# One attention stage in place of three: gathered rows kept in SBUF, softmax in blocks of seven items, radial network in the last stage

## The chip, the cores and the metric

The kernel runs on one core of one Trainium2 chip. The metric is device microseconds of one execution, the median over runs. The core's engines are TensorE (PE), VectorE (DVE), ScalarE (ACT), GpSimd (POOL, which issues the indirect DMAs) and SyncE (SP, which issues the plain ones). Each runs its own instructions in order; they meet only at semaphores.

## The reference

Four graph layers over 100,000 nodes of 128 numbers and 50,000 edges, each followed by a residual sum and a layer norm. Layer 1 (the attention) and layer 3 (the radial network) are what the change touches:

```python
# layer 1, per edge: score, softmax over the edges of one receiver, weighted sum
e = jnp.sum(Q[receiver] * K[sender], axis=-1) * scale
m = jax.ops.segment_max(e, receiver, num_segments=num_nodes)
w = jnp.exp(e - m[receiver])
denom = jax.ops.segment_sum(w, receiver, num_segments=num_nodes)
numer = jax.ops.segment_sum(w[:, None] * V[sender], receiver, num_segments=num_nodes)
return x + numer / denom @ Wo
...
# layer 3, per edge: a small network of the edge's length gives 4 x 32 weights for its message
h = jax.nn.silu(emb @ mlp_w0 + mlp_b0)
h = jax.nn.silu(h @ mlp_w1 + mlp_b1)
w = (h @ mlp_w2 + mlp_b2).reshape(-1, 4, MUL)
...
m0 = w[:, 0] * ss                                  # and m1, m2, m3, from w, the sender's row and the edge's direction
msg_s = jax.ops.segment_sum(mid_s, receivers, num_segments=num_nodes)
```

The edges come sorted by receiver, so a sum or a maximum over one receiver's edges is a scan along the edges that restarts where the receiver changes.

## The kernel before, in words

The edges are padded to 392 chunks of 128. Four chunks are an *item* (98 items), two items are an *eight* or a *pair* (49). The kernel is a row of stages, with a barrier of all engines between them: `prepare`, `scores_and_sort`, `gat_softmax`, `gat_sums`, `first_layer`, `attention_scores`, `attention_softmax`, `second_layer`, `gcn_first`, `gcn_second`, `final_edges`.

Inside a stage each engine runs `pipeline(engine, (f, lag), ...)`: in *slot* s it calls the listed functions in their order, each f for item s - lag. There is no scheduler; this order in a slot, the lags and the semaphores alone decide who waits for whom. `wait_item(engine, sems, t, u, back)` makes a step of item q wait until item q - back has passed a semaphore, which is how a buffer is protected: back 2 for two buffers, back 1 for one.

- `attention_scores` (tiles `asc_`): per item POOL gathers four chunks of sender rows (L1554), PE turns and multiplies the receiver rows (L1584, L1591), DVE takes their product with the gathered rows (`dot`, L1643 to L1648), SP stores the gathered rows to the table `xsrc`. Beside this the radial network is computed: PE `first`, `second`, `third` (L1597, L1603, L1610), two Silu on ACT (L1628, L1633), DVE `keep` (L1653), and a store to the table `radial`.
- `attention_softmax` (`asm_`): the softmax over all 50,176 scores at once, through a table in DRAM; meanwhile the line of flags `cont` (1 where an edge has the same receiver as the one before it) is broadcast into all partitions as `K["cont"]`.
- `second_layer` (`ats_`): per eight SP loads the rows of `xsrc`, POOL weights them (L1764), PE turns them, DVE scans (L1812), PE multiplies (L1785), ACT copies out, POOL adds the node's own row (L1769), DVE and ACT do the layer norm (`norm_measure`, `norm_root`, `norm_scale`, `apply`).
- `final_edges` (`mss_`): per item POOL gathers four chunks (L2110) and, 15 slots later, scatters four chunks to the output (L2102). ACT scales, PE turns (L2123), ACT copies, PE projects into `up` (L2130), DVE makes messages (`messages`, L2191 to L2198) with the weights loaded from `radial`, PE turns them (L2138), ACT copies them (`copy_msg`, L2173), PE reduces (L2145), DVE scans (L2205), PE turns back into `op` (L2152), DVE combines (L2211) and norms.

In `final_edges` the orders in a slot are, before the change:

```python
pipeline(pe, (turn_x, 1), (turn_back, 9), (project, 3), (reduce, 7), (turn_sums, 5))
pipeline(act, (copy_x, 2), (copy_msg, 6), (lambda t, u: norm_root(norm, act, t, u), 11), (scale_x, 0),
         (lambda t, u: norm_apply(norm, act, t, u, scattered, 64), 12))
pipeline(dve, (scan, 8), (messages, 4), (combine, 10), (lambda t, u: norm_scale(norm, dve, t, u), 11))
```

Of the kernel before, what the change touches and what calls it, by code (L numbers as in the profile page):

```python
# [20 lines left out]
P = 128  # L21
N = 100000
# [1499 lines left out]
def attention_scores(nc, A, T, K):  # L1522
    with ExitStack() as ctx:
        sb, ps, sem, sems, owned = stage_makers(nc, ctx, "asc")
        xs = [sb(f"xs{u}", [P, 4, ROW1]) for u in range(BUFS)]
        xd = [sb(f"xd{u}", [P, 4, D]) for u in range(BUFS)]
        xdT = [sb(f"xdT{v}", [P, 4, P]) for v in range(2)]
        prod = [sb(f"prod{u}", [P, 4, D]) for u in range(BUFS)]
        four_scores = [sb(f"fs{u}", [P, 4]) for u in range(BUFS)]
        scores = sb("scores", [P, CHUNKS])  # L1530
        rows = sb("rows", [P, 4, P])
        h1 = [sb(f"h1{v}", [P, 2, P]) for v in range(2)]
        h2 = [sb(f"h2{v}", [P, 2, P]) for v in range(2)]
# [4 lines left out]
        sT = ps("sT", [P, 4, P])
        loaded, gathered, turned, copied = sems("loaded"), sems("gathered"), sems("turned"), sems("copied")
        multiplied, dotted, kept, stored = sems("multiplied"), sems("dotted"), sems("kept"), sems("stored")  # L1540
        h1_ready, h1_done, h2_ready, h2_done = sems("h1_ready"), sems("h1_done"), sems("h2_ready"), sems("h2_done")
        wp_ready, w_ready, w_stored = sems("wp_ready"), sems("w_ready"), sems("w_stored")
        all_scored, scores_turned, rows_ready, rows_stored = sem("all_scored"), sem("scores_turned"), sem("rows_ready"), sem("rows_stored")
        block = ctx.enter_context(nc.Block())

        @block.gpsimd
        def _(pool):
            for q in range(ITEMS):
                t, u = q // BUFS, q % BUFS
                wait_item(pool, kept, t, u, 4)  # L1550
                wait_item(pool, stored, t, u, 4, 16)
                for j in range(4):
                    c = 4 * q + j
                    pool.indirect_dma_start(xs[u][:, j, :], None, T["t12"][0:EP + N],  # L1554
                                            bass.IndirectOffsetOnAxis(K["idx_a"][:, c:c + 1], 0)).then_inc(gathered[u], 16)

        @block.sync
        def _(sp):
            def store(t, u):
                sp.wait_ge(gathered[u], 64 * t + 64)  # L1560
                sp.dma_start(tile_rows(T["xsrc"], t, u), as_tile_rows(xs[u][:])).then_inc(stored[u], 16)

            def load(t, u):
                wait_item(sp, turned, t, u, 4)
                sp.dma_start(xd[u][:], part_rows(T["t12"][0:EP], t, u)).then_inc(loaded[u], 16)

            def store_w(t, u):
# [756 lines left out]
```

## Time and profile before

| what | us |
|---|---|
| median of 3 runs (lowest, highest) | 5378.56 (5373.77, 5383.27) |
| the profiled execution, its own time | 5376.34 |
| its span, first to last instruction | 5374.6 |
| `attention_scores` (2490 to 2989 in the span) | 499 |
| `attention_softmax` (2989 to 3023) | 34 |
| `second_layer` (3023 to 3321) | 298 |
| `gcn_first` (3321 to 3829) | 508 |
| `final_edges` (4353 to 5374) | 1021 |

The stages are cut at the first and last instruction on their own tiles. In a table of stretches, "busy" is the union of an engine's instructions, so an engine may be busy half of a stage and still set its pace through one chain; the busy shares say which engine cannot be the limit, the waits and the order of time say which is. Times in the timelines are us from the span's start; an instruction's duration may overlap the start of the next on its engine by about a tenth, so what a step costs is read from start to start.

### The profile page before, as it was taken

What the parts mean: (1) busy time and instruction counts of PE and PEld (TensorE: products, weight loads), DVE (VectorE), ACT (ScalarE), POOL (GpSimd) and SP (SyncE); (2) the same over time, 40 slices, a digit from 0 to 9 for tenths busy, and PEclk for the clock granted to TensorE, in tenths of its full rate; (3) what the DMA queues carried; (4) which work ended last, traced back from release to release, by engine and by line L of the source; (5) the groups of instructions that cost most, each with busy time, mean ns of one, the idle gap of its engine ahead of it and who ended that gap; (6) DMA issues with size and microseconds to landing.
All of it is one profiled execution on the core that took longest, in us unless ns stands there. A gap on an engine that the chain in (4) does not pass through costs nothing. (4 is left out here: it accounts for less than half of the span.)

```text
span 5374.6 us, 74716 instructions
## 1 busy us (share of the span) xinstructions
PE 3172.1 (59%) x15690; PEld 2478.5 (46%) x15690; DVE 3358.4 (62%) x11850; ACT 2679.9 (50%) x6869; POOL 3855.3 (72%) x3733
## 2 busy tenths in 40 slices
PE   3536555545534664465777465666788866655564
PEld 3536545524323442355666454455455544444442
DVE  6587555568877775575333696333477767666665
ACT  0106666648866886385222375333355554444443
POOL 5777777667766777487777576777677767777777
PEclk9555555579977887798999787888655578888887
DMA  2327777768845775366777786777677643333332
GB/s 73 77 73 225 241 239 238 227 152 250 251 145 160 225 225 180 113 205 194 212 213 214 243 286 206 210 212 212 180 209 208 204 134 101 98 97 98 97 97 74
DMA packets 846208, 953.70 MB, mean 177 GB/s; under 512 B 161164, under 2 KB 570097, under 8 KB 845827
## 3 DMA queue, kind: packets, MB, share of 16 engines
q1 hardware_dynamic: 730304, 765.68, 44.9%
q0 software_dynamic: 112896, 179.36, 14.4%
q10 hardware_dynamic: 2882, 7.36, 0.4%
q8 instruction: 33, 0.54, 0.0%
q14 instruction: 93, 0.76, 0.0%
HBM read 534.20 MB, written 423.34 MB: 178 GB/s over the span
## 5 line engine op out<-in xcount | busy, mean ns | idle before, releaser
L1035 POOL DMA_INDIRECT t_alpha<-gsm_raw,gsm_edge_idx x392 | 386.2, 985 | 165.7 <-issue 118.3
L2110 POOL DMA_INDIRECT mss_xs<-t_x,kept_idx_a x392 | 377.9, 964 | 143.9 <-issue 119.1
L2102 POOL DMA_INDIRECT out_dram<-mss_o,kept_scat_idx x392 | 395.0, 1008 | 119.4 <-issue 117.9
L534 POOL DMA_INDIRECT sort_xd<-in_x_dram,kept_dst_idx x392 | 379.2, 967 | 140.3 <-issue 118.5
L1966 POOL DMA_INDIRECT gs_xs<-t_z,kept_idx_a x392 | 380.5, 971 | 137.5 <-issue 119.2
L1025 POOL DMA_INDIRECT gsm_raw<-t_al,kept_idx_b x392 | 378.2, 965 | 124.1 <-issue 118.9
L1554 POOL DMA_INDIRECT asc_xs<-t_t,kept_idx_a x392 | 370.0, 944 | 134.2 <-issue 110.3
L1856 POOL DMA_INDIRECT gs_xs<-t_t,kept_idx_b x392 | 370.0, 944 | 133.2 <-issue 119.2
L536 POOL DMA_INDIRECT sort_xs<-in_x_dram,kept_src_idx x392 | 379.7, 969 | 119.4 <-issue 118.5
L1227 PE MATMUL gsm_hp<-kept_w,gsm_zT 128*128 128x128 f32 x1568 | 254.9, 311 | 353.5 <-ACT gsm_zT L1093 353.4
L216 PE MATMUL gs_tp<-kept_ident,gs_xs 128*128 128x128 f32 x784 | 271.6, 364 | 250.9 <-DMA gs_xs<-t_t,kept_idx_b 185.1
L1227 PEld LDWEIGHTS gsm_hp<-kept_w,gsm_zT 128*128 128x128 f32 x1568 | 214.6, 212 | 404.1 <-ACT gsm_zT L1093 404.0
L2162 ACT ACTIVATE mss_xk<-mss_xs 128x128 f32<-128x128 f32 x392 | 125.2, 390 | 515.8 <-DMA mss_xs<-t_x,kept_idx_a 515.8
L1433 ACT ACTIVATE gsm_o<-gsm_y,gsm_nb,gsm_rs 128x128 f32<-128x128 f32 x784 | 323.7, 490 | 24.9 <-issue 24.6
L755 PE MATMUL sort_tpd<-kept_ident,sort_xd 128*128 128x128 f32 x392 | 108.9, 433 | 384.7 <-DMA sort_xs<-in_x_dram,kept_src_idx 384.7
L1923 DVE TENSOR_TENSOR_SCAN gs_sc<-kept_cont,gs_sc,gs_tp 128x512 f32<-128x512 f32 (+1 forms) x98 | 125.4, 1279 | 308.8 <-PE gs_tp L217 308.8
L1433 ACT ACTIVATE sort_o<-sort_x,sort_nb,sort_rs 128x128 f32<-128x128 f32 x792 | 312.3, 489 | 0.0
L2123 PE MATMUL mss_xtp<-kept_ident,mss_xk 128*128 128x128 f32 x392 | 82.9, 350 | 382.7 <-ACT mss_xsT L2168 361.5
L216 PEld LDWEIGHTS gs_tp<-kept_ident,gs_xs 128*128 128x128 f32 x784 | 145.5, 186 | 352.1 <-DMA gs_xs<-t_t,kept_idx_b 223.6
L2205 DVE TENSOR_TENSOR_SCAN mss_sc<-kept_cont,mss_sc,mss_rp 128x512 f32<-128x512 f32 (+1 forms) x98 | 125.4, 1279 | 280.8 <-PE mss_rp L2145 280.7
L793 ACT COPY sort_al<-sort_sps 128x16 f32<-128x16 f32 x98 | 16.8, 171 | 551.0 <-PE sort_sps L765 551.0
L1912 ACT ACTIVATE gs_o<-gs_hp,kept_dlast2B 128x128 f32<-128x128 f32 x392 | 112.1, 369 | 313.6 <-PE gs_hp L1897 313.5
(536 smaller groups left out, 11243.8 us busy)
## 6 DMA issues: line engine op xcount, KB each, us to landing
t_t<-sort_o SPq DMA_DIRECT2D x66, 792.0 KB
t_x<-gsm_o SPq DMA_DIRECT2D x196, 264.0 KB
sort_x<-in_x_dram SPq DMA_DIRECT2D x66, 768.0 KB
gsm_x<-t_t SPq DMA_DIRECT2D x196, 256.0 KB
t_z<-gsm_z SPq DMA_DIRECT2D x196, 256.0 KB
out_dram<-gsm_o SPq DMA_DIRECT2D x196, 256.0 KB
t_t<-l_o SPq DMA_DIRECT2D x49, 528.0 KB, 3.1
t_xsrc<-asc_xs SPq DMA_DIRECT2D x98, 264.0 KB, 2.3
```

The costliest lines, as they stand in the source:

```text
L216: pe.matmul(out, lhsT=a, rhs=ident[:], start=True, stop=False, is_transpose=True)
L534: pool.indirect_dma_start(xd[u][:, j, :], None, A["x"], bass.IndirectOffsetOnAxis(K["dst_idx"][:, c:c + 1], 0)).then_inc(gathered[u], 16)
L536: pool.indirect_dma_start(xs[u][:, j, :], None, A["x"], bass.IndirectOffsetOnAxis(K["src_idx"][:, c:c + 1], 0)).then_inc(gathered[u], 16)
L1025: pool.indirect_dma_start(raw[:, c, 0:HEADS], None, T["al"], bass.IndirectOffsetOnAxis(from_idx[:, c:c + 1], 0)).then_inc(gathered[u], 16)
L1035: pool.indirect_dma_start(T["alpha"], bass.IndirectOffsetOnAxis(edge_idx[:, c:c + 1], 0), raw[:, c, :], None).then_inc(scattered[u], 16)
L1227: mm = pe.matmul(hp[u % 2][:, j, :], zT[u][:, j, :], K["w1"][:], start=True, stop=True)
L1433: ac = act.activation(norm["o"][u][:, g, :], norm["y"][u][:, g, :], ACT.Identity, bias=norm["nb"][u][:, g:g + 1], scale=norm["rs"][u][:, g ...
L1554: pool.indirect_dma_start(xs[u][:, j, :], None, T["t12"][0:EP + N], bass.IndirectOffsetOnAxis(K["idx_a"][:, c:c + 1], 0)).then_inc(gathere ...
L1856: pool.indirect_dma_start(xs[u][:, j, :], None, T["t12"], bass.IndirectOffsetOnAxis(K["idx_b"][:, c:c + 1], 0)).then_inc(gathered[u], 16)
L1966: pool.indirect_dma_start(xs[u][:, j, :], None, T["z1"], bass.IndirectOffsetOnAxis(K["idx_a"][:, c:c + 1], 0)).then_inc(gathered[u], 16)
L2102: pool.indirect_dma_start(T["out"], bass.IndirectOffsetOnAxis(K["scat_idx"][:, c:c + 1], 0), o[u][:, j, :], None, bounds_check=N - 1, oob_ ...
L2110: pool.indirect_dma_start(xs[u][:, j, :], None, T["x3"], bass.IndirectOffsetOnAxis(K["idx_a"][:, c:c + 1], 0)).then_inc(gathered[u], 16)
```

## The change

Three stages become one, `attention` (tiles `att_`), and the radial network moves into `final_edges`.

- The gathered rows stay in a ring of 20 tiles `xs`; `xsrc` is neither stored nor loaded. POOL only gathers.
- The softmax runs in 14 blocks of seven items. In each, eight small steps on DVE alternate with six on PE and one Exp on ACT, one step per slot, with a running maximum and a running sum carried from block to block.
- The aggregation (weight, turn, scan, multiply, combine, norm) runs 16 slots behind the gather. Weighting is on ACT (was on POOL), adding the own row is on DVE (was on POOL), in one instruction per chunk with the division by the denominator.
- `in_slots` replaces `pipeline` there: parts are (f, lag, every, count).
- `K["cont"]` is filled in `gcn_first`, by four broadcasts on ACT's queue, and `gcn_first` loads its own flags item by item.
- In `final_edges` the three PE steps, the two Silu and `keep` join the slot; the load of `radial` goes. To make room in PSUM, `op` and `up` have one buffer each instead of two, so `turn_back` waits for the combine of the item before (back 1, was 2) and `project` for the messages of the item before (back 1, was 2).

The diff, cut to its core:

```diff
+BLOCK = 7
+RING = 20
+FIRST_STEP = BLOCK + 1
+WEIGHT_LAG = FIRST_STEP + 8
+def in_slots(*parts):
+    for s in range(max(lag + every * (count - 1) for _, lag, every, count in parts) + 1):
+        for f, lag, every, count in parts:
+            if s >= lag and (s - lag) % every == 0 and (s - lag) // every < count:
+                f((s - lag) // every)
...
+# attention: PE
+            in_slots((turn_weights, FIRST_STEP + 7, BLOCK, BLOCKS), (turn_scores, FIRST_STEP + 1, BLOCK, BLOCKS),
+                     (turn_tops, FIRST_STEP + 2, BLOCK, BLOCKS), (turn_carried_tops, FIRST_STEP + 3, BLOCK, BLOCKS),
+                     (turn_sums, FIRST_STEP + 5, BLOCK, BLOCKS), (turn_carried_sums, FIRST_STEP + 6, BLOCK, BLOCKS),
+                     (attend, WEIGHT_LAG + 2, 1, ITEMS), (multiply, 1, 1, ITEMS), (turn, 0, 1, ITEMS),
+                     (turn_weighted, WEIGHT_LAG, 1, ITEMS))
+# attention: ACT
+            in_slots((exponents, FIRST_STEP + 4, BLOCK, BLOCKS), (weight, WEIGHT_LAG, 1, ITEMS), (copy, 0, 1, ITEMS),
+                     (root, WEIGHT_LAG + 4, 2, PAIRS), (apply, WEIGHT_LAG + 5, 2, PAIRS))
+# attention: DVE
+            in_slots((take_weights, FIRST_STEP + 7, BLOCK, BLOCKS), (dot, 2, 1, ITEMS), (scan, WEIGHT_LAG + 1, 1, ITEMS), (combine, WEIGHT_LAG + 2, 1, ITEMS),
+                     (measure, WEIGHT_LAG + 3, 2, PAIRS), (scale, WEIGHT_LAG + 4, 2, PAIRS),
+                     (find_flags, FIRST_STEP, BLOCK, BLOCKS), (scan_tops, FIRST_STEP + 1, BLOCK, BLOCKS), (scan_row_tops, FIRST_STEP + 2, BLOCK, BLOCKS),
+                     (shift, FIRST_STEP + 3, BLOCK, BLOCKS), (scan_sums, FIRST_STEP + 4, BLOCK, BLOCKS),
+                     (scan_row_sums, FIRST_STEP + 5, BLOCK, BLOCKS), (invert_sums, FIRST_STEP + 6, BLOCK, BLOCKS))
...
 # gcn_first
+            part = EP // 4
+            for k in range(4):
+                act.dma_start(K["cont"][:, k * part:(k + 1) * part], T["cont"][0:1, k * part:(k + 1) * part].broadcast_to([P, part])).then_inc(cont_loaded, 16)
...
 # final_edges
-        op = [ps(f"op{v}", [P, 4, D]) for v in range(2)]
+        op = ps("op", [P, 4, D])
+        hp, wp = ps("hp", [P, 4, P]), ps("wp", [P, 4, D])
-        up = [ps(f"up{v}", [P, 4, D]) for v in range(2)]
+        up = ps("up", [P, 4, D])
             def project(t, u):
                 pe.wait_ge(x_copied[u], t + 1)
-                wait_item(pe, msg_ready, t, u, 2)
+                wait_item(pe, msg_ready, t, u, 1)
             def turn_back(t, u):
                 pe.wait_ge(scanned[u], t + 1)
-                wait_item(pe, combined, t, u, 2)
+                wait_item(pe, combined, t, u, 1)
+            def radial_first(t, u):
+                wait_item(pe, h2_done, t, u, 1)
+                for pair in range(2):
+                    mm = pe.matmul(hp[:, pair, :], K["m0g"][:, 2 * (u % 2) + pair, :], radial_block(K, t, u), start=True, stop=True)
+                mm.then_inc(h1_ready[u], 1)
-            pipeline(pe, (turn_x, 1), (turn_back, 9), (project, 3), (reduce, 7), (turn_sums, 5))
+            pipeline(pe, (radial_second, 1), (turn_x, 1), (turn_back, 9), (project, 3), (radial_third, 2), (radial_first, 0), (reduce, 7), (turn_sums, 5))
+            def radial_one(t, u):
+                act.wait_ge(h1_ready[u], t + 1)
+                act.activation(h1[u % 2][:], hp[:, 0:2, :], ACT.Silu, bias=K["mb0"][:, 0:1]).then_inc(h1_done[u], 1)
-            pipeline(act, (copy_x, 2), (copy_msg, 6), (lambda t, u: norm_root(norm, act, t, u), 11), (scale_x, 0),
+            pipeline(act, (radial_two, 1), (copy_x, 2), (radial_one, 0), (copy_msg, 6), (lambda t, u: norm_root(norm, act, t, u), 11), (scale_x, 0),
                      (lambda t, u: norm_apply(norm, act, t, u, scattered, 64), 12))
-            pipeline(dve, (scan, 8), (messages, 4), (combine, 10), (lambda t, u: norm_scale(norm, dve, t, u), 11))
+            pipeline(dve, (scan, 8), (messages, 4), (keep, 3), (combine, 10), (lambda t, u: norm_scale(norm, dve, t, u), 11))
```

The order on ACT in one slot of `final_edges`, before the change (`mss_xsT` is `copy_x`, `mss_mT` `copy_msg`, `mss_sd` the norm's root, `mss_xk` `scale_x`, `mss_o` the norm's apply):

```order
L2168 COPY mss_xsT<-mss_xtp 128x512
L2173 COPY mss_mT<-mss_tp 128x512 x2
L1408 ACTIVATE mss_sd<-mss_mv,kept_eps 128x4
L2162 ACTIVATE mss_xk<-mss_xs 128x128 x4
L1433 ACTIVATE mss_o<-mss_y,mss_nb,mss_rs 128x128 x4
```

and after it (L2247 is `radial_two`, L2242 `radial_one`):

```order
L2247 ACT_TABLE_LOAD
L2247 ACTIVATE mss_h<-mss_hp,kept_mb 128x256
L2233 COPY mss_xsT<-mss_xtp 128x512
L2242 ACTIVATE mss_h<-mss_hp,kept_mb 128x256
L2238 COPY mss_mT<-mss_tp 128x512 x2
L1408 ACT_TABLE_LOAD
L1408 ACTIVATE mss_sd<-mss_mv,kept_eps 128x4
L2227 ACTIVATE mss_xk<-mss_xs 128x128 x4
L1433 ACTIVATE mss_o<-mss_y,mss_nb,mss_rs 128x128 x4
```

Silu and the root alternate in every slot now, and each of the two is preceded by a load of ACT's function table; `radial_one` stands ahead of `copy_msg` and of the root.

The order on PE in one slot of `final_edges`, before (`mss_xtp` is `turn_x`, `mss_op` `turn_back`, `mss_up` `project`, `mss_rp` `reduce`, `mss_tp` `turn_sums`):

```order
L2123 MATMUL mss_xtp<-kept_ident,mss_xk 128x128 x4
L2152 MATMUL mss_op<-kept_ident,mss_sc 128x128 x4
L2130 MATMUL mss_up<-kept_wup,mss_xsT 128x128 x4
L2145 MATMUL mss_rp<-mss_mT,kept_wout 128x512 x2
L2138 MATMUL mss_tp<-kept_ident,mss_msg 128x128 x8
```

and after (L2210 is `radial_second`, L2217 `radial_third`, L2205 `radial_first`):

```order
L2210 MATMUL mss_hp<-mss_h,kept_m 128x256
L2171 MATMUL mss_xtp<-kept_ident,mss_xk 128x128 x4
L2200 MATMUL mss_op<-kept_ident,mss_sc 128x128 x4
L2178 MATMUL mss_up<-kept_wup,mss_xsT 128x128 x4
L2217 MATMUL mss_wp<-kept_m,mss_h 128x256 x2
L2205 MATMUL mss_hp<-kept_emb,kept_m0g 128x128 x2
L2193 MATMUL mss_rp<-mss_mT,kept_wout 128x512 x2
L2186 MATMUL mss_tp<-kept_ident,mss_msg 128x128 x8
```

`radial_third` and `radial_first` stand between `project` and `reduce`, behind `turn_back`, which waits for DVE.

## Rows read from the trace of the kernel before

**Rows 1.** Part 1 of the page: busy time and share of each engine

```profile
PE 3172.1 (59%) x15690; PEld 2478.5 (46%) x15690; DVE 3358.4 (62%) x11850; ACT 2679.9 (50%) x6869; POOL 3855.3 (72%) x3733
```

**Rows 2.** Stretches by stage: length, busy of each engine, TensorE clock, DMA share, GB/s

```profile
2490.00:2989.00 499.00, 357.71 (x2160) 314.78 (x2160) 182.80 (x1079) 140.90 (x295) 370.03 (x392) 0.92 0.75 210
2989.00:3023.00 34.00, 4.92 (x12) 2.17 (x12) 18.41 (x41) 1.81 (x2) 0.00 (x0) 0.50 0.53 207
3023.00:3321.00 298.00, 175.90 (x1176) 164.08 (x1176) 258.74 (x935) 210.91 (x491) 206.24 (x98) 0.83 0.79 267
4353.00:5374.00 1021.00, 584.27 (x2744) 441.81 (x2744) 627.33 (x2059) 438.80 (x1176) 772.88 (x784) 0.82 0.33 96
```

**Rows 3.** Part 5 of the page, costliest groups: busy, mean ns, idle before, releaser

```profile
L2110 POOL DMA_INDIRECT mss_xs<-t_x,kept_idx_a x392 | 377.9, 964 | 143.9 <-issue 119.1
L2102 POOL DMA_INDIRECT out_dram<-mss_o,kept_scat_idx x392 | 395.0, 1008 | 119.4 <-issue 117.9
...
L1554 POOL DMA_INDIRECT asc_xs<-t_t,kept_idx_a x392 | 370.0, 944 | 134.2 <-issue 110.3
```

**Rows 4.** Timeline of DVE, early in the final stage (start, duration)

```profile
4419.95 1.28 DVE L2205 TENSOR_TENSOR_SCAN mss_sc<-kept_cont,mss_sc,mss_rp 128x512 f32<-128x512 uint8 x1
...
4424.02 0.68 DVE L2211 TENSOR_TENSOR mss_y<-mss_y,mss_op 128x512 f32<-128x512 f32 x1
...
4426.26 0.17 DVE L1419 RECIPROCAL mss_rs<-mss_sd 128x4 f32<-128x4 f32 x1
...
4426.58 1.28 DVE L2205 TENSOR_TENSOR_SCAN mss_sc<-kept_cont,mss_sc,mss_rp 128x512 f32<-128x512 uint8 x1
```

**Rows 5.** Timeline of PE, and DVE's next scan, one slot of the final stage

```profile
4709.35 1.06 PE L2123 MATMUL mss_xtp<-kept_ident,mss_xk 128*128 128x128 f32 x4 [4.24 <-ACT mss_xsT L2168]
...
4710.20 1.06 PE L2152 MATMUL mss_op<-kept_ident,mss_sc 128*128 128x128 f32 x4
...
4711.05 1.90 PE L2130 MATMUL mss_up<-kept_wup,mss_xsT 128*128 128x128 f32 x8
...
4712.76 1.91 PE L2145 MATMUL mss_rp<-mss_mT,kept_wout 128*128 128x512 f32 x4
...
4714.79 1.28 DVE L2205 TENSOR_TENSOR_SCAN mss_sc<-kept_cont,mss_sc,mss_rp 128x512 f32<-128x512 f32 x1 [3.63 <-PE mss_rp L2145]
```

**Rows 6.** Groups of the old attention_scores: `keep` on DVE, Silu on ACT

```profile
L1653 DVE TENSOR_TENSOR asc_w<-asc_wp,kept_mb 128x512 f32<-128x512 f32 x98 | 67.6, 690 | 27.1 <-PE asc_wp L1610 20.1 <-issue 6.3
...
L1628 ACT ACTIVATE asc_h<-asc_hp,kept_mb 128x256 f32<-128x256 f32 x98 | 46.5, 474 | 95.6 <-PE asc_hp L1597 94.7 <-issue 0.9
```

**Rows 7.** Timeline of PE, radial third and first in the old attention_scores

```profile
2605.98 1.28 PE L1610 MATMUL asc_wp<-kept_m,asc_h 128*128 128x256 f32 x4 [1.91 <-DVE asc_w L1653]
...
2613.65 0.61 PE L1597 MATMUL asc_hp<-kept_emb,kept_m0g 128*128 x4
```

**Rows 8.** Timeline of ACT around a table load, in gat_softmax

```profile
1739.83 0.58 ACT L1088 COPY gsm_xT<-gsm_tp 128x512 f32<-128x512 f32 x1
1740.43 1.28 ACT L1433 ACT_TABLE_LOAD   x1
1741.72 1.65 ACT L1433 ACTIVATE gsm_o<-gsm_y,gsm_nb,gsm_rs 128x128 f32<-128x128 f32 x4
```

**Rows 9.** Timeline of ACT, copy of the messages and root, final stage

```profile
4424.24 1.08 ACT L2173 COPY mss_mT<-mss_tp 128x512 f32<-128x512 f32 x2
4426.38 0.30 ACT L1408 ACTIVATE mss_sd<-mss_mv,kept_eps 128x4 f32<-128x4 f32 x1 [1.07 <-DVE mss_mv L1399]
```

**Rows 10.** Timeline of DVE, first and last of a dot, old attention_scores

```profile
2702.91 0.29 DVE L1643 CUSTOM_DVE_ANT_0 asc_prod<-asc_qp,asc_xs 128x128 f32<-128x128 f32 x1 [1.69 <-DMA asc_xs<-t_t,kept_idx_a]
...
2704.10 0.17 DVE L1648 TENSOR_TENSOR asc_scores<-asc_fs,asc_xs 128x4 f32 x1
```

**Rows 11.** Timeline of DVE, one eight of second_layer

```profile
3150.35 1.64 DVE L1382 BATCH_NORM_STATS2 ats_small<-ats_y 128x6 f32<-128x128 f32 x8
...
3153.07 2.35 DVE L1812 TENSOR_TENSOR_SCAN ats_sc<-kept_cont,ats_sc,ats_tp 128x1024 f32<-128x1024 f32 x1
...
3155.94 1.64 DVE L1382 BATCH_NORM_STATS2 ats_small<-ats_y 128x6 f32<-128x128 f32 x8
```

More of the change, by code:

```diff
@@ L1538, in attention_scores @@
[L1538 to L1543, printed above, removed]
+        block_scores = [sb(f"bs{v}", [P, ROWS]) for v in range(2)]
@@ L1792, in apply, with exponents, root @@
+            def exponents(b):
+                act.wait_ge(soft_v, V_STEPS * b + 4)
+                act.activation(e[:], shifted[:], ACT.Exp).then_inc(exped, 1)
+            def root(p):
+                norm_root(norm, act, p // BUFS, p % BUFS)
+            def apply(p):
+                t, u = p // BUFS, p % BUFS
                 act.wait_ge(norm["scale_ready"][u], t + 1)
@@ L1815, in measure, with dot @@
-            def measure(t, u):
-                dve.wait_ge(summed[u], t + 1)
-                norm_measure(norm, dve, t, u)
-            def scale(t, u):
+            link = chain_of(dve, chain_v)
+            def dot(q):
+                dve.wait_ge(multiplied, q + 1)
+                dve.wait_ge(gathered[q % RING], 64 * (q // RING) + 64)
+                rows = xs[q % RING]
+                for j in range(4):
+                    dt = dve.tensor_tensor_reduce(prod[q % 2][:, j, :], qp[q % 2][:, j, :], rows[:, j, 0:D], 1.0, 0.0, ALU.mult, ALU.add,
+                                                  four_scores[q % BUFS][:, j:j + 1])
+                dt.then_inc(dotted, 1)
+                dve.wait_ge(dotted, q + 1)
+                dve.tensor_copy(kB[:, 4 * q:4 * q + 4], rows[:, :, D])
+                place = 4 * (q % BLOCK)
+                dve.tensor_tensor(block_scores[q // BLOCK % 2][:, place:place + 4], four_scores[q % BUFS][:], rows[:, :, D], ALU.mult).then_inc(kept, 1)
@@ L1825, in _ @@
-            dve.wait_ge(zero_set, 1)
-            pipeline(dve, (measure, 5, EIGHTS), (scan, 2, EIGHTS), (scale, 5, EIGHTS))
+            for v in range(2):
+                dve.memset(o[v][:, :, D:ROW1], 0.0).then_inc(o_set, 1)
+            dve.memset(zeros[:], 0.0)
+            dve.memset(ones[:], 1.0)
+            dve.memset(shifted[:], 0.0)
+            dve.memset(top_ahead[:], -BIG)
+            dve.memset(top_back[:], -BIG)
+            dve.memset(last_sum[:], 0.0)
+            link(dve.memset(sc[BUFS - 1][:], 0.0))
@@ L1839, in gcn_first @@
         o = [sb(f"o{u}", [P, 4, D]) for u in range(BUFS)]
+        goes = [sb(f"goes{u}", [P, 4 * P], mybir.dt.uint8) for u in range(BUFS)]
         tp = [ps(f"tp{v}", [P, 4, P]) for v in range(2)]
```

521 lines of the change are left out of this document (266 added, 255 removed).

## The prediction

> **What bounds the kernel now.** I read the page's busy times first, then a table of stretches by stage, then in each stage that the change touches the groups and the timeline. Over the whole span POOL is busiest, 72% [rows 1], but it is bound only in some stages. In `attention_scores` POOL issues 392 gathers; each is 0.94 us and nearly all the idle time before them is issue, so the stage runs at the gather's pace: (370.0 + 134.2) / 98 = about 5.1 us an item [rows 3], with DVE busy 183 of 499 us [rows 2]. `attention_softmax` is a chain of small steps, 34 us with no engine busy for more than 18. In `second_layer` DVE is busy 259 of 298 us [rows 2], and its timeline runs from one eight to the next in 5.59 us almost without a gap [rows 11]: DVE is the bound. `final_edges` is POOL's again: 784 indirect DMAs, and (377.9 + 143.9 + 395.0 + 119.4) / 98 = 10.6 us an item with the start [rows 3]; the stage's length over 98 is 10.4 [rows 2]. There PE waits 4.2 us in each slot and DVE 3.6 [rows 5], which is the room into which the radial network is moved. How much room there is when POOL does not wait shows early in that stage: DVE's scan comes every 6.63 us [rows 4].
>
> **Part one: the attention.** Removed are 499 + 34 + 298 = 831 us [rows 2]. The new stage has three stretches. A slot is one item.
>
> DVE's work in a full slot. The dot of an item: 2704.10 - 2702.91 + 0.1 = 1.3 us [rows 10]. The scan of 512: 4421.23 less the overlap of a tenth, 1.2 [rows 4]. Combine in four pieces of 128: a quarter of 0.68 each plus some 0.05 for being four instructions, 0.8 (bound above: four times 0.29, a DVE instruction of this width with two operands [rows 10], 1.2) [rows 4]. Measure and scale of a pair: 5.59 less the scan's 2.3 = 3.3, of which scale is 0.6 (3155.94 less 3153.07 and 2.3) and measure 2.7 [rows 11]. The softmax steps have no row of their own: some 29 small DVE instructions in a block of seven; at 0.17, the small ones of these rows [rows 4, 10], 4.9 us, at 18.41 / 41 = 0.45, those of the old softmax that are 392 wide [rows 2], 13. They are 28 rows of 128, between the two, and about one us for the hand-over to PE and back before `take_weights` comes on top: I take 8.4, or 1.2 a slot (0.7 to 1.9). Sum: 1.3 + 1.2 + 0.8 + 1.65 + 1.2 = 6.2 us, above the gather's 5.1. So DVE, not POOL, sets the pace once the aggregation is running, if nothing waits.
>
> Something waits. `scale` of a pair (every other slot) needs the root of the same slot on ACT, which stands behind `copy`, which needs PE's `turn`, which stands behind the small transposes of the softmax step, `attend` and `multiply`; and the small transposes need the softmax step with which DVE ended the slot before. From that end: 0.15 + 0.5 for small transposes + attend and multiply, each 1.71 at the low clock, as project takes [rows 5], 0.85 at the high one + turn 0.85 or 0.43 [rows 5] + copy 0.58 [rows 8] + root 0.3 [rows 9] + 0.2 of hand-overs = 3.4 to 6.0, and I take 4.8, between the clocks. DVE alone reaches this point after 3.3. So an even slot takes 4.8 + 0.6 + 1.0 = 6.4 to 6.9 and an odd one 3.3 + 2.7 + 1.0 = 7.0; a table load (Exp against Sqrt, 1.29 [rows 8]) falls into one slot in seven, and `take_weights` stalls in one, 0.3 together. I take 7.1 us a slot, 6.3 and 7.7 as ends.
>
> The stage: 17 slots of gather alone, 6 + 17 x 5.1 = 92; three as the aggregation starts, 16; 80 full slots at 7.1, 568; then the 16 slots of lag without dot and multiply, where DVE has 1.2 + 0.8 + 1.65 and for seven slots a softmax step: 7 x 5.7 + 7 x 3.9 = 67; last norm and store 12. Sum 755. The gain is 831 - 755 = **76 us** (with 6.3: 140; with 7.7: 28). Transfers don't decide: `xsrc` and `radial` are no longer moved, and DMA was at 0.75 to 0.79 [rows 2] at a faster pace. POOL may run four items ahead of the weighting, so a slower DVE stops it without being stopped itself.
>
> **Part two: `gcn_first`.** Its 6.3 MB broadcast was beside the softmax's chain, now it lies beside gathers. At that stretch's 207 GB/s [rows 2] it is 30 us of transfer; nothing if it goes into free DMA time, 30 if gathers wait for all of it. Four items of buffer (20 us of gathers) stand against it: I take 5. The item-wise flags (64 KB) are a quarter of one of the other loads, nothing.
>
> **Part three: the radial network in `final_edges`.** Its instructions are small beside the room: on DVE 0.6 (0.69 less the overlap), on ACT 2 x 0.4 [rows 6], on PE about 2. But two single buffers and the order turn the room into a chain. Follow slot s. PE's `turn_back` (item s-9) waits for DVE's combine of item s-10, which DVE does in this same slot behind scan, messages and keep; before, it waited for the combine a slot earlier. Behind it on PE stand project, `radial_third`, `radial_first` and reduce. ACT's `radial_one` of item s waits for `radial_first` in the same slot, and behind it on ACT stand `copy_msg`, a table load and the root. DVE's `scale` waits for that root, and behind it stands the next slot's scan. Nothing of this overlaps. One turn:
>
> - DVE, scan to the end of combine: 4424.02 + 0.68 - 4419.95 = 4.75 [rows 4], plus keep 0.6 [rows 6]: 5.35
> - to PE, 0.12 as from reduce's end (4714.67) to the scan at 4714.79 [rows 5]
> - turn_back 0.85, project 1.71 [rows 5]
> - `radial_third` 1.2 (1.28 [rows 7]), `radial_first` 0.45 (0.61 less overlap at the high clock [rows 7])
> - to ACT 0.05; `radial_one` 0.38 (0.47 less the overlap) [rows 6], `copy_msg` 1.08, root 0.30 [rows 9]
> - the table load: from the copy's end 1740.41 to the next instruction at 1741.72, 1.31 [rows 8]
> - to DVE 0.1, `scale` 0.32, from the reciprocal to the next scan [rows 4]
>
> Sum 5.35 + 0.12 + 2.56 + 1.65 + 0.05 + 1.76 + 1.31 + 0.42 = **13.2 us** against 10.4. Reduce (1.8) ends well inside ACT's part. PE then has turn_sums, the second product and turn_x, and stands idle about 4 us till the combine, as it does now [rows 5]; after such a pause turn_back and project run at 1.2 GHz now (0.21 and 0.43 us a product), and reduce, 3.4 us after the restart, at 2.4 (0.85 for 512 columns) [rows 5]. So I price the first two at the low clock and the third across the change. All at the high clock would be 1.7 less, 11.5; all low 14.0.
>
> The Trainium skill ("ScalarE: Activation LUTs", "What ACT_TABLE_LOAD costs") gives about 1.28 us for the load plus about 1.38 for a drain at every switch of set. The row agrees with the load (1.28) and not with the drain: the next instruction starts 0.01 us after it, and only 0.02 lie ahead of it [rows 8]. With the page's figure the turn would be 14.6. The same page ("Table sets: the hidden batching unit") says to batch by set, which this order does not; how it would cost here is the chain above.
>
> The stage: slots 0 to 9, before combine and root join, 69 us (6 to the first gathered item, six at about 5.3, two at 6.5, two at 9); 88 full slots x 13.2 = 1162; the drain 67, as first the radial steps and table loads, then messages, drop out (10.9, 10.8, 9.9, 7.6, four at 4.7, 9 for the last); the last scatter 8. Sum 1306 against 1021 [rows 2]: **+285 us**. With a turn of 11.5 it is +135, with 14.0 +355.
>
> **Sum**: -76 + 5 + 285 = +214 on the profiled execution's own 5376.3 (its span 5374.6 and 1.7 around it), 5590. That execution is 2.2 us under the median of the three, no difference. About 0.2%, 11 us, is what a measurement can tell from no change.
>
> **Rivals.**
> - *The clock stays high in the chain.* PE works in a third of the chain's turn and more beside it. It was granted 0.82 in this stage [rows 2] and the low level just where the chain would need it [rows 5], against it. Turn 11.5: -76 + 5 + 135, 5440.
> - *A switch of table costs twice its row.* The rows show the load ahead of an apply [rows 8], not ahead of this root; if as much again as 1.31 us lies around it here, the turn is 14.5 and 88 x 1.31 come on top: 5705. Against it: nothing but 0.02 us lies around it where it can be seen. The drain of the Trainium skill's page above would be this case.
> - *The attention gains nothing.* If the waits among its small softmax steps add more than 1 us a slot to 7.1, the stage takes 831 again: 5666. For it: six round trips between DVE and PE in a block. Against it: all but one are a slot apart.
> - *POOL still paces the last stage* (the other side). If combine is never late, because DVE needs only 7.2 us of 10.4, the chain does not form: then -76 + 5, 5305. It decides at a turn of 10.4: the chain would have to be 2.8 us shorter than its rows. The order speaks against it: each link waits for the one before in the same slot.
> - *DVE in the attention is cheaper and the gather paces it*: 98 x 5.1 + 80, 580 instead of 755, which with +285 gives 5415.
>
> **How the numbers follow.** The chain at the low clock 0.55, at the high one 0.14, with dearer table switches 0.07, attention without gain 0.1, POOL's pace 0.08, attention at the gather's pace 0.06. The likeliest gives 5590. The range leaves out the POOL case and the dearest one and takes in the high clock and an attention without gain: 5425 to 5700. Slower holds for all but POOL's pace and a share of the combinations of high clock and cheap attention: slower 0.87, same 0.03, faster 0.10.
>
> **What would show it.** In the profile after: the final stage at about 1300 us, POOL's gathers there waiting for ACT, DVE's `scale` waiting for the root, ACT's `radial_one` for PE, about 196 table loads at 1.28. PE's turn_back waiting for DVE's combine. The attention at about 750 with DVE the busiest, above 80%, its `scale` waiting for the root, POOL waiting for ACT's weighting. I am wrong if POOL shows only issue ahead of its gathers in the last stage, if table loads are hidden behind waits (then `radial_one` was not late), or if DVE in the attention has long waits for PE other than before `take_weights` and `scale`.

## The result, and the profile after

The changed kernel takes 5649.83 us, the median of 4 runs (5644.23 to 5659.9), against 5378.3 before: a ratio of 1.0507, with an interval of 1.0489 to 1.0525. The forecast was 5590, with a range of 5425 to 5700. The profiled execution took 5644.23, its span is 5642.5.

The first view is part 1 of the page, which answers to [rows 1]: busy time of each engine, its share of the span, and its instructions.

```profile
PE 3337.4 (59%) x15856; PEld 2596.3 (46%) x15856; DVE 3544.0 (63%) x12659; ACT 3015.1 (53%) x7424; POOL 3641.6 (65%) x3635
```

POOL has 98 instructions less and works 214 us less, ACT works 335 us more, and no engine is busier than 65%. More work in total is no explanation: the span grew by 268 us while the busiest engine lost time. The table of stretches says where it went. Its columns are those of [rows 2]; the stretches are the new attention stage (and inside it the part where every step runs), `gcn_first`, `gcn_second`, and `final_edges` with its start, its middle and its end apart.

```profile
2490.00:3232.00 742.00, 446.75 (x2534) 403.83 (x2534) 579.12 (x2765) 371.45 (x971) 371.23 (x392) 0.72 0.52 152
2620.00:3100.00 480.00, 300.19 (x1783) 275.77 (x1783) 407.33 (x1948) 263.55 (x691) 270.85 (x287) 0.77 0.57 168
3232.00:3747.00 515.00, 326.57 (x1764) 238.22 (x1764) 188.60 (x197) 165.94 (x490) 370.02 (x392) 0.87 0.82 226
3747.00:4270.00 523.00, 450.91 (x1372) 264.19 (x1372) 376.90 (x1378) 280.56 (x882) 378.92 (x392) 0.56 0.67 199
4270.00:4400.00 130.00, 84.45 (x392) 64.05 (x392) 55.33 (x151) 54.71 (x129) 68.67 (x73) 0.79 0.19 48
4400.00:5500.00 1100.00, 685.38 (x3066) 526.12 (x3067) 569.50 (x1774) 638.47 (x1285) 632.27 (x646) 0.75 0.20 54
5500.00:5642.50 142.50, 63.41 (x267) 44.50 (x265) 68.76 (x233) 60.99 (x136) 65.20 (x66) 0.72 0.16 47
```

The attention takes 742 us where the three stages took 831 [rows 2], so 89 less; `gcn_first` 515 where it took 508, 7 more; `gcn_second` 523 where it took 524, 1 less. `final_edges` takes 130 + 1100 + 142.5 = 1372.5 us where it took 1021 [rows 2], 351 more. The sum, -89 + 7 - 1 + 351, is the 268 us of the span. In the middle of the last stage every engine is idle for over 35% of the time. That points at a chain of waits, not at a bound of one engine.

The list of waits of that stage has for each wait the engine and line, whom it waited for, the sum in us, how often, and the longest:

```profile
ACT mss_h L2242 <- PE mss_hp L2205: 539.1, 97, 7.7
DVE mss_rs L1419 <- ACT mss_sd L1408: 523.8, 87, 6.3
...
PE mss_xtp L2171 <- ACT mss_xsT L2233: 452.6, 97, 5.1
POOL out_dram L2150 <- ACT mss_o L1433: 349.4, 92, 11.0
```

Each engine waits for another about once an item: ACT's `radial_one` for PE's `radial_first`, DVE's `norm_scale` for the root, POOL for ACT. All that was in the forecast, except that it is POOL's scatters that wait for ACT (349 us) and hardly its gathers (26 us in the stage). The third row was not: PE waits in `turn_x` (L2171), for ACT's `copy_x`. Of the wait that the forecast named, PE's `turn_back` for DVE's combine, there are 35 us in the whole stage.

One turn in the timeline shows why (start, duration, in brackets the idle time before):

```profile
4980.78 0.47 ACT L2242 ACTIVATE mss_h<-mss_hp,kept_mb 128x256 f32<-128x256 f32 x1 [5.89 <-PE mss_hp L2205]
4981.15 1.06 ACT L2238 COPY mss_mT<-mss_tp 128x512 f32<-128x512 f32 x2
4982.23 1.28 ACT L1408 ACT_TABLE_LOAD   x1
...
4983.53 0.30 ACT L1408 ACTIVATE mss_sd<-mss_mv,kept_eps 128x4 f32<-128x4 f32 x1
4983.73 1.26 ACT L2227 ACTIVATE mss_xk<-mss_xs 128x128 f32<-128x128 f32 x4
4983.86 0.18 DVE L1419 RECIPROCAL mss_rs<-mss_sd 128x4 f32<-128x4 f32 x1 [5.81 <-ACT mss_sd L1408]
...
4984.27 1.28 DVE L2278 TENSOR_TENSOR_SCAN mss_sc<-kept_cont,mss_sc,mss_rp 128x512 f32<-128x512 f32 x1
4984.90 1.63 ACT L1433 ACTIVATE mss_o<-mss_y,mss_nb,mss_rs 128x128 f32<-128x128 f32 x4
...
4986.55 1.28 ACT L2247 ACT_TABLE_LOAD   x1
...
4987.84 0.47 ACT L2247 ACTIVATE mss_h<-mss_hp,kept_mb 128x256 f32<-128x256 f32 x1
...
4988.22 0.58 ACT L2233 COPY mss_xsT<-mss_xtp 128x512 f32<-128x512 f32 x1
...
4988.94 1.09 PE L2171 MATMUL mss_xtp<-kept_ident,mss_xk 128*128 128x128 f32 x4 [5.08 <-ACT mss_xsT L2233]
4989.05 0.68 DVE L2284 TENSOR_TENSOR mss_y<-mss_y,mss_op 128x512 f32<-128x512 f32 x1
...
4989.88 1.09 PE L2200 MATMUL mss_op<-kept_ident,mss_sc 128*128 128x128 f32 x4
...
4990.76 1.91 PE L2178 MATMUL mss_up<-kept_wup,mss_xsT 128*128 128x128 f32 x8
...
4992.46 1.35 PE L2217 MATMUL mss_wp<-kept_m,mss_h 128*128 128x256 f32 x4
...
4993.65 0.61 PE L2205 MATMUL mss_hp<-kept_emb,kept_m0g 128*128 x4
...
4994.29 0.47 ACT L2242 ACTIVATE mss_h<-mss_hp,kept_mb 128x256 f32<-128x256 f32 x1 [5.50 <-PE mss_hp L2205]
```

From one `radial_one` to the next it is 13.51 us. ACT has no gap in it from 4980.78 to 4988.80: its whole slot, both table loads included, 8.0 us. Then PE's `turn_x` starts, because the one buffer `xtp` is only free when `copy_x` has read it. Behind it in PE's order stand `turn_back`, `project`, `radial_third` and `radial_first`, for which `radial_one` waits. The forecast's own chain is there too: DVE's combine ends at 4989.73, and `turn_back` starts at 4989.88, just when PE is done with `turn_x`. So **two chains are of one length within about 0.15 us**: the forecast's, through DVE (scan to combine) and half of ACT's slot, and a second, through all of ACT's slot and no DVE. The trace gives the wait to the second.

In the attention, DVE is the busiest (407 of 480 us, 85%). The groups of that stretch:

```profile
L1836 DVE SCALAR_TENSOR_TENSOR att_y<-att_hp,att_rdB,att_own 128x128 f32<-128x128 f32 x276 | 76.4, 339 | 4.6 <-PE att_hp L1659 3.9
...
L1421 DVE RECIPROCAL att_small<-att_sd 128x8 f32<-128x8 f32 x35 | 7.3, 210 | 47.7 <-ACT att_sd L1408 47.5
```

69 items have 276 combines of 339 ns, and most of DVE's idle time, 47.5 of 73 us, is the wait of `scale` for the root on ACT.

### The profile page after: what moved, and what is told of

The parts are those of the page before. It is cut to its first block and busy times, and to the rows that moved or that the text cites. A ratio compares the mean times of both kernels' runs of the same rounds, so it can differ in the third digit from the quotient of the medians.

```text
span 5642.5 us, 74512 instructions
## 1 busy us (share of the span) xinstructions
PE 3337.4 (59%) x15856; PEld 2596.3 (46%) x15856; DVE 3544.0 (63%) x12659; ACT 3015.1 (53%) x7424; POOL 3641.6 (65%) x3635
## 5 line engine op out<-in xcount | busy, mean ns | idle before, releaser
L1592 POOL DMA_INDIRECT att_xs<-t_t,kept_idx_a x392 | 371.2, 947 | 256.2 <-ACT att_xw L1719 135.1
L2171 PE MATMUL mss_xtp<-kept_ident,mss_xk 128*128 128x128 f32 x392 | 102.9, 415 | 458.5 <-ACT mss_xsT L2233 452.6
L1419 DVE RECIPROCAL mss_rs<-mss_sd 128x4 f32<-128x4 f32 x98 | 17.4, 178 | 523.9 <-ACT mss_sd L1408 523.8
L2242 ACT ACTIVATE mss_h<-mss_hp,kept_mb 128x256 f32<-128x256 f32 x98 | 46.5, 474 | 539.1 <-PE mss_hp L2205 539.1
L1971 DVE TENSOR_TENSOR_SCAN gs_sc<-gs_goes,gs_sc,gs_tp 128x512 f32<-128x512 uint8 x98 | 125.4, 1279 | 316.0 <-PE gs_tp L217 316.0
L2171 PEld LDWEIGHTS mss_xtp<-kept_ident,mss_xk 128*128 128x128 f32 x392 | 67.7, 210 | 496.0 <-issue 482.0
```

What stands on the lines that cost most here:

```text
L1592: pool.indirect_dma_start(xs[q % RING][:, j, :], None, T["t12"][0:EP + N], bass.IndirectOffsetOnAxis(K["idx_a"][:, c:c + 1], 0)).then_inc( ...
```

## The experiments

Two chips were used, and each kernel is compared with runs of the kernel before on its own chip (5391.65 us for experiments 1, 2, 3 and 8, 5379.48 for 4 to 7). Ratios are what to compare. Where a mean turn between 4400 and 5200 is given, it is the mean distance of DVE's scans there; "from start to start" is from an instruction group's first start to the next group's.

**1. The attention alone.** The new attention and `gcn_first` with the `final_edges` of before. The radial network is left out: the weights that `final_edges` loads are rows of the table `xdst`, as many bytes.

```diff
+            def load(t, u):
+                wait_item(sp, msg_ready, t, u, 4)
+                sp.dma_start(as_tile_rows(wt[u][:]), tile_rows(T["xdst"], t, u)).then_inc(wt_loaded[u], 16)
...
-            pipeline(pe, (radial_second, 1), (turn_x, 1), (turn_back, 9), (project, 3), (radial_third, 2), (radial_first, 0), (reduce, 7), (turn_sums, 5))
+            pipeline(pe, (turn_x, 1), (turn_back, 9), (project, 3), (reduce, 7), (turn_sums, 5))
```

> The new attention and gcn_first with the final stage of the kernel before (two buffers for op and up, no radial network in it). The radial network is left out altogether: the weights loaded there are the rows of another table of the same shape. Theory: the whole loss is in the final stage, and attention gains what its own stretch shows (740 against 831 us, gcn_first 8 us more), so 5378 - 91 + 8 = 5295, faster by 1.5%. Rival: the attention's gain is eaten elsewhere (its rows in SBUF and its loads disturb the neighbours), then within 0.3% of 5378.

Measured: 5305.95 us, ratio 0.9838 (0.9822 to 0.9855). The attention, with what it costs in `gcn_first`, is worth 1.6%, and its last stage takes 1020 us, as before. So all of the loss is in the new `final_edges`.

**2. No table loads in the last stage.** Relu in place of Silu, which the trace then shows without any table load in that stage; the radial network's values are other ones.

```diff
-                act.activation(h1[u % 2][:], hp[:, 0:2, :], ACT.Silu, bias=K["mb0"][:, 0:1]).then_inc(h1_done[u], 1)
+                act.activation(h1[u % 2][:], hp[:, 0:2, :], ACT.Relu, bias=K["mb0"][:, 0:1]).then_inc(h1_done[u], 1)
...
-                act.activation(h2[u % 2][:], hp[:, 2:4, :], ACT.Silu, bias=K["mb1"][:, 0:1]).then_inc(h2_done[u], 1)
+                act.activation(h2[u % 2][:], hp[:, 2:4, :], ACT.Relu, bias=K["mb1"][:, 0:1]).then_inc(h2_done[u], 1)
```

> The changed kernel with Relu in place of both Silu of the final stage: the same instructions, but no table load. Part of the computation changed: the radial network's activation. Theory A (the chain of the prediction: DVE scan to combine, PE turn_back to radial_first, ACT radial_one to root, DVE scale): one load is in it, the turn falls from 13.5 to 12.2 and the time by about 88 x 1.3 = 115 us, to 5535. Theory B (the turn is all of ACT's slot plus PE's turn_x to radial_first): both loads are in it, the turn falls by 2.6 to 10.9 and the time by 230, to 5420. If both chains are there, the longer one is left: 12.1 to 12.2. With a drain besides each load (1.3 us more each) A would give 230 and B 460.

Measured: 5582.26, ratio 1.0358 (1.034 to 1.0375). The scans of DVE are now 11.89, 13.28, 12.95 and 13.08 us apart, in rotation: 12.80 in the mean between 4400 and 5200, where the changed kernel has 13.66. The waits in that stretch:

```profile
PE mss_xtp L2171 <- ACT mss_xsT L2233: 136.4, 63, 2.2
PEld mss_op L2200 <- issue: 128.5, 63, 2.5
PE mss_op L2200 <- DVE mss_y L2284: 112.8, 63, 2.3
```

From `radial_one` to `copy_x` ACT now takes 4.58 us instead of 7.44, so 2.9 less for two loads. `turn_x` therefore waits 2.2 us instead of 5, and `turn_back` waits for combine each time: the DVE chain has become the longer one, as it must when two chains tie and the other is shortened more. In the DVE chain there was one load, and from `radial_one` to the scan it is 2.20 us instead of 3.60. By that alone the turn should have been 12.25. The rest is in PE's timeline:

```profile
4905.46 1.08 PE L2200 MATMUL mss_op<-kept_ident,mss_sc 128*128 128x128 f32 x4 [1.77 <-DVE mss_y L2284]
4906.34 1.92 PE L2178 MATMUL mss_up<-kept_wup,mss_xsT 128*128 128x128 f32 x8
4908.05 1.91 PE L2217 MATMUL mss_wp<-kept_m,mss_h 128*128 128x256 f32 x4
4909.75 1.06 PE L2205 MATMUL mss_hp<-kept_emb,kept_m0g 128*128 x4
4910.60 2.13 PE L2193 MATMUL mss_rp<-mss_mT,kept_wout 128*128 128x512 f32 x4
```

Here third and first run at 1.2 GHz too: the granted clock is 0.50 from 4908.05 to 4910.60, and they take 1.70 and 0.85 from start to start. In the changed kernel's row above it was granted 0.73 in third and 1.00 in first, which took 1.19 and 0.44. Third is as slow as this in three turns of four (first takes 0.59 to 0.85 there); in the fourth it takes 0.98. In the mean between 4400 and 5200 the two take 1.53 and 0.67, against 1.22 and 0.44 in the changed kernel: 0.54 us more, which is the difference.

**3. The DVE chain opened alone.** `turn_back` moved behind `reduce`, so that nothing of the radial network stands behind DVE's combine.

```diff
-            pipeline(pe, (radial_second, 1), (turn_x, 1), (turn_back, 9), (project, 3), (radial_third, 2), (radial_first, 0), (reduce, 7), (turn_sums, 5))
+            pipeline(pe, (radial_second, 1), (turn_x, 1), (project, 3), (radial_third, 2), (radial_first, 0), (reduce, 7), (turn_back, 9), (turn_sums, 5))
```

> The changed kernel with turn_back moved behind reduce in PE's order of the final stage, so that project, radial_third, radial_first and reduce no longer stand behind the combine of the slot. Theory A: project then waits for messages only, and the chain loses keep, combine and turn_back: 13.5 - 2.2 = 11.2 to 11.4, 190 us less, 5460. Theory B: only turn_back (0.9) drops out of the turn: 12.6, 80 us less, 5570.

Measured: 5623.22, ratio 1.0426 (1.0408 to 1.0443), a gain of 0.8% on the changed kernel's 1.0507; had the DVE chain been the only one, it would have been about 3.5% (theory A above). The wait for ACT is still there, between 4400 and 5200:

```profile
PE mss_xtp L2171 <- ACT mss_xsT L2233: 275.3, 60, 4.7
```

The four matmuls of `turn_back`, 0.9 us, are out of the ACT chain as well, and so are the turns in which it waited for DVE (0.2 us in the mean): the turn should have become 12.6. It is 13.3 to 13.4, again with PE at 1.2 GHz through project, third and first in most turns (1.71, 1.70, 0.86, at a granted clock of 0.50), where the changed kernel had third at 1.05 to 1.30. In the mean third and first take 0.77 us more together.

**4. The ACT chain opened alone.** `radial_one` moved to the end of ACT's slot, so that neither `copy_msg` nor the root stands behind it.

```diff
-            pipeline(act, (radial_two, 1), (copy_x, 2), (radial_one, 0), (copy_msg, 6), (lambda t, u: norm_root(norm, act, t, u), 11), (scale_x, 0),
-                     (lambda t, u: norm_apply(norm, act, t, u, scattered, 64), 12))
+            pipeline(act, (radial_two, 1), (copy_x, 2), (copy_msg, 6), (lambda t, u: norm_root(norm, act, t, u), 11), (scale_x, 0),
+                     (lambda t, u: norm_apply(norm, act, t, u, scattered, 64), 12), (radial_one, 0))
```

> The changed kernel with radial_one moved to the end of ACT's order in the final stage (behind the norm's apply); both table loads stay. ACT's root no longer stands behind the PE product of the same slot, so both A's and B's chain are cut. What is left is DVE scan to combine 5.35, PE turn_back, project, radial_third, radial_first, reduce 6.1, hand-overs 0.25: 11.7 us an item, 160 us less than the changed kernel, 5490. Rival: ACT's load by itself (8 us of work and two table loads a slot) or PE's bounds it; then nothing changes.

Measured: 5532.96, ratio 1.0281 (1.0264 to 1.0298). Both old chains are cut at `radial_one`, and a third remains, without ACT, between 4400 and 5200:

```profile
DVE mss_sc L2278 <- PE mss_rp L2193: 320.2, 65, 5.9
...
PE mss_op L2200 <- DVE mss_y L2284: 175.6, 65, 2.9
```

DVE's scan waits for PE's reduce, which stands behind `turn_back`, project, third and first, and `turn_back` waits for the combine behind the scan before. This is the loop that the expectation named, at 11.7 us. The scans are mostly 11.4 to 13.3 us apart, 12.35 in the mean; third and first, at 1.44 and 0.66 us in the mean instead of 1.2 and 0.45, are most of the difference.

**5. Both orders.** The edits of 3 and 4 together.

> Both changes of order together (turn_back behind reduce on PE, radial_one last on ACT). The longest chain left is DVE scan and messages 4.1, PE project to reduce 5.2 and hand-overs, 9.5 us, below POOL's 10.4: the final stage is back at POOL's pace, 1021 us and some 15 more at its start and end. 5650 - 353 + 15 = 5312, faster than the kernel before by 1.2%. Rival: the radial network's work itself is too much for the stage, whatever the order: 11 us an item or more, 5370 or above.

Measured: 5346.43, ratio 0.9935 (0.9919 to 0.9952). The turn in the body of the stage is 10.24 us, POOL's pace of before (10.27), though each item has all of the radial network and as many table loads as before the edits. Between 4400 and 5200 the list has none of POOL's waits but `issue`:

```profile
POOL out_dram L2150 <- issue: 94.7, 306, 1.7
POOL mss_xs L2158 <- issue: 93.5, 307, 0.3
```

The groups of ACT in that stage:

```profile
L2242 ACT ACT_TABLE_LOAD x88 | 112.9, 1283 | 1.6
L1408 ACT ACT_TABLE_LOAD x88 | 112.9, 1283 | 1.6
```

So 226 us of table loads cost the pace nothing once the order lets them lie beside POOL's DMAs. Against the changed kernel the edits of 3 and 4 take 0.8 and 2.3 per cent of the time before when made apart, and 5.7 together (1.0507 - 0.9935). The stage takes 1070 us, 49 above before, at an equal pace, and the traces put all of that at its start. The eleventh scan comes 160.6 us into the stage, against 106.9 before; from there to the end it is 909.4 us, against 914.9. In the first slots POOL only gathers, which is half of its work, and the scans were 6.6 us apart there before. Here they are 10.2 to 10.5 apart, and the gathers wait for ACT's `scale_x`, as the 46 us from 4340 to 4386 show:

```profile
POOL mss_xs L2158 <- ACT mss_xk L2227: 20.1, 4, 7.4
```

So a loop among the other engines of about POOL's own length is left in this order too, not one of 9.5 us as expected. It costs nothing where POOL has its full work and 54 us where it has half. Which steps it runs through was not followed out.

**6. The root first in the attention.** `root` ahead of `weight` and `copy` on ACT.

```diff
-            in_slots((exponents, FIRST_STEP + 4, BLOCK, BLOCKS), (weight, WEIGHT_LAG, 1, ITEMS), (copy, 0, 1, ITEMS),
-                     (root, WEIGHT_LAG + 4, 2, PAIRS), (apply, WEIGHT_LAG + 5, 2, PAIRS))
+            in_slots((exponents, FIRST_STEP + 4, BLOCK, BLOCKS), (root, WEIGHT_LAG + 4, 2, PAIRS), (weight, WEIGHT_LAG, 1, ITEMS), (copy, 0, 1, ITEMS),
+                     (apply, WEIGHT_LAG + 5, 2, PAIRS))
```

> The changed kernel with the norm's root moved ahead of weight and copy in ACT's order of the attention stage. Theory: DVE waits for that root 53 us in all (34 times) because it stands behind the copy, which waits for PE; ahead of them it is ready a slot earlier, and as DVE is the stage's bound, 40 to 50 us go: 5605. Rival: the wait only stands in for another one (the next is PE's attend or the weighting), then less than 15 us.

Measured: 5600.1, ratio 1.0411 (1.0394 to 1.0428), about 1% or 50 us less than the changed kernel. The attention takes 690 us, and DVE's wait for the root is gone from its list.

**7. All three orders.** The edits of 5 and 6.

> All three changes of order together. The stages are apart, so the gains add: the time of both orders less that of root first, 5312 - 45 = 5267, faster than the kernel before by 2.1%. If the root's wait only stands in for another: 5300.

Measured: 5290.19, ratio 0.9834 (0.9818 to 0.9851). This beats both kernels: 1.7% faster than before, a small gain but clear of the spread, and 6.4% faster than the changed one. The 2.1% expected is missed mostly by the slow start of the last stage seen in experiment 5 (here the eleventh scan comes at 156.6 us, against 106.9 before). Its stretches, the attention and the last stage:

```profile
2490.00:3181.00 691.00, 433.50 (x2534) 394.43 (x2534) 575.76 (x2765) 372.73 (x973) 370.66 (x392) 0.73 0.57 163
4217.00:5283.30 1066.30, 774.97 (x3724) 589.57 (x3724) 695.07 (x2157) 755.69 (x1548) 778.47 (x784) 0.84 0.27 68
```

The attention has the same instructions as in the change and takes 691 us instead of 742, the last stage 1066 instead of 1372.

**8. The single buffers alone.** The kernel before with one buffer each for `op` and `up`.

```diff
-        op = [ps(f"op{v}", [P, 4, D]) for v in range(2)]
+        op = [ps("op", [P, 4, D])] * 2
...
-                wait_item(pe, combined, t, u, 2)
+                wait_item(pe, combined, t, u, 1)
```

> The kernel before with one buffer instead of two for op and up in its final stage (waits one item back), and no radial network there. Theory: single buffers alone make a turn of DVE scan to combine 4.75 + PE turn_back, project, reduce 4.4 + 0.25 = 9.4 us, inside POOL's 10.4, so nothing changes: within 0.3% of 5378. Rival: the loss of the second buffers is the cause by itself; then the final stage goes to 12 us an item or more, 5530 or above.

Measured: 5406.19, ratio 1.0027 (1.0018 to 1.0037). `turn_back` does wait for combine there, 289 us between 4400 and 5300, and yet it costs only 15 us: the wait replaces another one of PE (342 us in the same stretch before, in `turn_x`). In the two profiles the cost is again at the start, where POOL only gathers: the scans are 9.9 us apart where they were 6.6, and the eleventh comes 143.1 us into the stage instead of 106.9, of which the rest of the stage gets back half (896.8 us instead of 914.9). So the single buffers do close a loop of 9.9 us, which POOL's 10.3 covers. They are not the cost in the changed kernel; what was put behind the wait is.

## Why the prediction was right, and where it was off

**Sign and mechanism.** The forecast said that the last stage stops being POOL's and becomes a chain of PE, ACT and DVE in one slot, at 13.2 us. It is one: the mean distance of scans over the 88 full slots is (5543.92 - 4344.55) / 88 = 13.63 us. Experiments 3 to 5 show by the order alone, with the same instructions, that it is a chain: it goes away, and with it 302 of the 351 us by which the stage had grown. The rival in which POOL still paces the stage failed for the reason given.

**The step that failed** is "PE then has turn_sums, the second product and turn_x, and stands idle about 4 us till the combine". PE stands idle 5 us, but ahead of `turn_x`, till `copy_x`. I followed `turn_x` as work that fits into the pause, and did not ask when its own release comes: `copy_x` stands behind `radial_two` in ACT's next slot, and that behind scale_x, apply and a second table load. Thus the second load, which I counted nowhere, is in this chain. From start to start in the timeline above, in us: radial_one 0.37, copy_msg 1.08, load 1.30, root 0.20, scale_x 1.17, apply 1.65, load 1.29, radial_two 0.38, copy_x 0.72 with the hand-over, and on PE turn_x 0.94, turn_back 0.88, project 1.70, third 1.19, first 0.64 with the hand-over: 13.51 us. Experiment 2 (the wait moves from one to the other) and experiment 3 (the wait of `turn_x` stays) show it. The size came out nearly right by luck: the chain that I had left out happens to tie with the one that I had. One part of "What would show it" failed with this step: `turn_back` hardly waits for combine (35 us).

**Terms of the sum for the last stage**, 1306 forecast, 1372.5 measured:

- the start to the tenth slot 69, measured 4344.55 - 4270 = 74.6: +5.6
- 88 full slots at 13.2, measured at 13.63: +37. A turn by its rows is 13.51. In one slot of four the scans are 14.13 apart and in the next 13.39; ahead of that late scan the timeline has a gap of 0.55 marked issue. There `turn_back` does wait for combine, some 0.4 us, and from one of ACT's `radial_one` to the next this turn takes 13.90 where the others take 13.51 to 13.62
- the end 75 with the scatter, measured 5642.5 - 5543.92 = 98.6: +24. The next four scans are 11.45, 12.45, 10.43 and 8.98 apart where I had 10.9, 10.8, 9.9 and 7.6, 4 us more, and the last three 4.39 each where I had 4.7. The other 20 us lie behind the last scan, at 5600.40: 42.1 where I had left 21.7. I priced the last slots by the steps that were left in them, without POOL, which sets the pace there: its scatters follow each other every 1.29 us, so 5.15 an item, from 5595.55 to the last one:

```profile
5630.30 0.98 POOL L2150 DMA_INDIRECT out_dram<-mss_o,kept_scat_idx  x1 [0.31 <-issue]
5631.59 0.99 POOL L2150 DMA_INDIRECT out_dram<-mss_o,kept_scat_idx  x1 [0.30 <-issue]
```

**The clock in the chain.** I took turn_back and project at the low level and third across the change. The rows agree: project takes 1.70 from start to start at a granted clock of 0.50 (1.2 GHz), third 1.19 at 0.73, across the change, and first 0.44 at 1.00 (2.4 GHz). Third at the low level throughout takes 1.70, in experiment 2. The rival "the clock stays high" failed.

**The table load.** The row above shows 1.28 for the load at 4982.23 and the root at 4983.53, 0.02 after its end. A drain of about 1.38 us at every switch, as the Trainium skill has it ("ScalarE: Activation LUTs", "What ACT_TABLE_LOAD costs"), is not seen here either, and the rival built on it failed. The stage has 176 loads, where I said about 196: in the slots at either end only one kind of function is left. The same page of the Trainium skill says to batch activation calls by set ("Table sets: the hidden batching unit"). Experiment 2 shows what batching could have won at most with the order of the change, 1.5%; in experiment 5 the unbatched loads cost the pace nothing.

**The attention**: forecast 755, measured 742, and the gain 89 instead of 76. A full slot took (3134.52 - 2594.37) / 78 = 6.92 by the scans, against 7.1. The parts are off in both directions. Combine in four pieces takes 1.1 us a slot (76.4 / 69) where I took 0.8; the upper bound, 1.2, was the better row. The hand-over before `take_weights` stalls DVE 0.5 us in the mean of ten blocks, not about 1, as one block shows:

```profile
2901.00 0.94 DVE L1807 RECIPROCAL att_rden<-att_run 28x128 f32<-28x128 f32 x1
2902.34 0.19 DVE L1812 COPY att_rdB<-att_soft 128x28 f32<-128x28 f32 x1 [0.40 <-PE att_soft L1663]
```

DVE is busy 407 / 480 of a slot of 6.92, 5.9 us. By the lines of that stretch, over its 69 items, this is dot 1.1, scan 1.2, combine 1.1, norm 1.5 and the softmax steps 1.0, where I took 1.3, 1.2, 0.8, 1.65 and 1.2. That `scale` waits for the root was right: experiment 6 takes the wait away, and 52 of the stage's 742 us with it. Experiment 1 bears out the part as a whole. The rivals "the attention gains nothing" and "the gather paces it" both failed.

**`gcn_first`**: forecast +5, measured +7, with the DMA share up to 0.82 and 116.6 MB moved instead of 103.7. Half of these 12.9 MB are the item-wise flags and half the broadcast. The gathers say when the time goes: those of the sixth item start 30.8 us into the stage, against 25.5 before, and from there on to the last item they stay 5.3 to 5.4 behind. So 5 of the 7 us go in the first 31 us, where the broadcast runs, and the flags, loaded all along the stage, cost its pace nothing, as forecast. No run has one without the other.

**What stays open**: which steps make up the loop of 10.2 to 10.5 us that shows at the start of the last stage in experiment 5, and whether a second buffer for `xtp` would do as much as another order. Neither was tried.

## What to carry to other kernels

When work is moved into the idle time of in-order engines, follow every wait of a slot to its own release, one slot back too, and compare all closed loops: here two tied, so that removing either alone gave 0.8% and 2.3%, and both together 5.7%. Idle time is only room for work if what stands behind that work is not waited for in the same slot. Look at the start and the end of a stage too, where the engine that paces its body has only half of its work: a loop that is covered in the body shows there. Try the order first: three lists put in another order, with not one instruction changed, turned a loss of 5.1% into a gain of 1.7%.

## What the runs showed of the hardware

Two results were not expected. When a wait in PE's slot became shorter (experiments 2 and 3), TensorE did not come back to 2.4 GHz earlier but later: third was at 1.2 GHz in most turns, and first in many. That gave back 0.54 us of the 1.4 won in experiment 2, and 0.77 of the 1.1 won in experiment 3. In the turn shown of the changed kernel the granted clock goes down in the pause ahead of `turn_x` and up again during third; what decides the moment was not tried. A chain that is estimated with the clock of the old order can be wrong by that much after an edit that touches no PE instruction at all, as in experiment 2. And in one slot of four DVE has a gap of 0.55 us marked issue ahead of its scan, with nothing in the profile that it waits for; by the rows here it adds about 0.1 us to the mean turn, and what it is was not found out.

A table load also costs a little more than its own 1.28 us. In experiment 2 the root starts 0.12 before the copy ahead of it ends (4912.16 against 4912.28); with the load in between there is no overlap, and 0.02 lie on either side of the load. From start to start a load costs 1.43 us there, half of the 2.86 that ACT's path became shorter.
